# Scores of two heads side by side: queries and keys as fp16 pairs of 64 rows in an attention kernel

## The reference

```python
q = heads(hidden_states @ W_q)                       # (8, 20, 512, 16)
k_t = heads(text_ehs @ W_k)                          # (8, 20, 508, 16)
v_t = heads(text_ehs @ W_v)
scores_t = jnp.einsum('bhsd,bhtd->bhst', q, k_t) * attn_scale
probs_t = jax.nn.softmax(scores_t, axis=-1)
text_out = jnp.einsum('bhst,bhtd->bhsd', probs_t, v_t)
qsem = _l2norm(jnp.einsum('bhst,bte->bhse', probs_t, text_ehs))
sem = jnp.einsum('bhse,bne->bhsn', qsem, _l2norm(ip_ehs))
fused = attn_scores + SEM_SCALE * sem                # attn_scores: q against the 4 image keys
probs_ip = jax.nn.softmax(fused, axis=-1) * spatial_mask[None, None, :, None]
out = (text_out + ip_out) @ W_out + b_out + residual
```

## Time and profile before

| what | value |
|---|---|
| median of three executions | 1642.24 us |
| the profiled execution, its own time | 1642.41 us |
| its span | 1640.5 us |
| mean granted TensorE clock | 0.982 |
| PE busy | 1569.2 us, 96% |
| DVE busy | 1303.0 us, 79% |
| POOL busy | 1258.8 us, 77% |
| ACT busy | 1078.8 us, 66% |
| first and last score matmul (L1593) | 285.0 and 1599.9 us |
| memory read and written by DMA | 68.51 and 34.55 MB |

### The profile page before, as it was taken

The page is one execution under the profiler, slowest core; times in us unless marked ns, Lnnn a source line. Parts: engine busy times, 40 slices in busy tenths (PEclk is TensorE's granted clock), DMA queues, the critical chain, the costliest instruction groups (busy, mean ns, idle before and its releaser), DMA issues.

```text
span 1640.5 us, 39314 instructions
## 1 busy us (share of the span) xinstructions
PE 1569.2 (96%) x13322; PEld 954.5 (58%) x13322; DVE 1303.0 (79%) x3181; ACT 1078.8 (66%) x2308; POOL 1258.8 (77%) x1187
## 2 busy tenths in 40 slices
PE   4999999999999999999999999999999999999996
PEld 2776667555555555555555555555555555555553
DVE  6455454688989977987799789977997899789975
ACT  4465555767777767766777677766776777677762
POOL 4233233788989978997899789977998799879982
PEclk9899999899999999999999999999999999999998
DMA  5455757778789879897889888887888788878973
GB/s 203 133 161 154 200 165 189 150 133 133 137 142 177 154 142 158 149 143 148 156 149 148 149 142 167 144 153 138 155 160 155 139 162 152 155 138 140 153 127 92
DMA packets 656043, 247.89 MB, mean 151 GB/s; under 512 B 619081, under 2 KB 645330, under 8 KB 655858
## 3 DMA queue, kind: packets, MB, share of 16 engines
q1 hardware_dynamic: 654658, 243.75, 77.7%
q10 hardware_dynamic: 1200, 1.80, 0.3%
HBM read 68.51 MB, written 34.55 MB: 63 GB/s over the span
## 4 chain that ended last, share of the span: by engine, by line
PE 76%; DVE 9%; issue 5%; ACT 3%; DMA 3%; POOL 3%; SPq 1%; DVEq 0%; ACTq 0%; POOLq 0%
PE bank L1636 26%; PE bank L1637 16%; PE bank L1689 13%; PE bank L1593 7%; PE bank L1641 3%; PE bank L1603 3%; DVE neg_max L1238 3%; PE bank L1635 3%; DVE probs L1250 2%; DMA late<-wkv 2%; PE bank L1666 2%; PE bank L1750 2%; ACT probs L864 1%; POOL wkv L745 1%; PE bank L1676 1%
## 5 line engine op out<-in xcount | busy, mean ns | idle before, releaser
L1636 PE MATMUL bank<-u_sb,late 127*128 127x508 f16 x2560 | 947.0, 376 | 0.0
L1637 PE MATMUL bank<-u_sb,late 127*128 127x508 f16 (+3 forms) x2560 | 763.9, 298 | 0.0
L1238 DVE TENSOR_REDUCE neg_max<-bank 128x1 f32<-128x508 f32 x640 | 434.3, 679 | 182.2 <-PE bank L1593 181.7
L1635 PE MATMUL bank<-v_ring,late 127*128 127x42 f16 x2560 | 468.0, 183 | 8.8 <-DMA late<-wkv 8.8
L745 POOL TENSOR_TENSOR wkv<-probs,wkv 128x508 f16<-128x508 f32 x320 | 365.4, 1147 | 103.7 <-ACT wkv L876 102.9
L1250 DVE SCALAR_TENSOR_TENSOR probs<-bank,probs 128x508 f32<-128x508 f32 x640 | 431.2, 674 | 5.8 <-PE bank L1637 5.8
L1635 PEld LDWEIGHTS bank<-v_ring,late 127*128 127x128 f16 x2560 | 247.1, 97 | 241.2 <-DMA late<-wkv 11.0
L1636 PEld LDWEIGHTS bank<-u_sb,late 127*128 127x128 f16 x2560 | 248.5, 97 | 187.4 <-issue 3.7
L853 ACT ACTIVATE exp_bias<-neg_max 128x1 f32<-128x1 f32 x512 | 103.8, 203 | 376.0 <-DVE neg_max L1238 373.4
L864 ACT ACTIVATE probs<-bank,exp_bias 128x508 f32<-128x508 f32 x512 | 341.0, 666 | 0.2
L752 POOL TENSOR_TENSOR probs<-probs,wkv 128x508 f32<-128x508 f32 x256 | 290.4, 1145 | 0.0
(11 more groups left out here) (199 smaller groups left out, 1894.9 us busy)
## 6 DMA issues: line engine op xcount, KB each, us to landing
raw<-k_parts SPq DMA_DIRECT2D x192, 79.4 KB, 3.8
raw<-in_ctx_cols SPq DMA_DIRECT2D x8, 1016.0 KB, 7.4
raw<-q_parts SPq DMA_DIRECT2D x32, 240.0 KB, 3.7
v_parts<-v_sb SPq DMA_DIRECT2D x8, 840.0 KB, 11.6
v_ring<-v_parts SPq DMA_DIRECT2D x32, 210.0 KB, 4.1
u_parts<-u_sb SPq DMA_DIRECT2D x8, 825.5 KB, 7.2
u_sb<-u_parts SPq DMA_DIRECT2D x8, 825.5 KB, 5.2
raw<-in_x_cols SPq DMA_DIRECT2D x8, 768.0 KB, 4.4
```

What stands on the lines that cost most here:

```text
L1238: nc.vector.tensor_reduce(neg_max[:, v % 4:v % 4 + 1], bank[s_bank(v)][:, 0:T], AX.X, ALU.max, negate=True)\
L1635: nc.tensor.matmul(o, hi_k, v_ring[0:TP, n, h, k, :], start=(k == 0), stop=False)
L1636: nc.tensor.matmul(y, hi_k, u_sb[0:TP, par, GH[k]:GH[k] + T], start=(k == 0), stop=False)
L1637: done = nc.tensor.matmul(y[:, k * TP:T], hi_k, u_sb[0:TP, par, UL[k]:UL[k] + U_COLS[k]], start=False, stop=(k == TT - 1))
```

## The change

Queries and keys are split into two fp16 parts instead of three bf16 parts. A product then needs four stacked blocks of 16 rows, 64 rows instead of 96. Head h and head h+10 lie in rows 0 to 63 and 64 to 127, and their scores are made by two matmuls in a row, one in each half of the array's rows, into the two score banks. Units now come in pairs: the same 128 query rows of heads h and h+10. So that both matmuls stand together, both wait for the exponentials of all earlier units.

The parts are now split without the scale of the inputs; the scale (`score_unit`, one number per batch) is applied in the exponential, and to the row maximum in the shift. The shift is made for every unit. In phase 1 the second split on ACT and the third on POOL go away, and the queries' parts are stored twice. Groups have four heads instead of five. The table set that holds both exp and log is loaded once by name, and the loads inside phase 2 are gone.

```diff
-    PAIRS = [(0, 0), (1, 0), (2, 0), (0, 1), (1, 1), (0, 2)]
-    KS = len(PAIRS) * D
+    KS = 4 * D
-    GROUP = 5
+    GROUP = 4
+    FAR = H // 2
+    PART_STORES = 3 * NC
...
+        def place(v):
+            pair, rest = divmod(v % OF_BATCH, 2 * ST)
+            return pair + rest % 2 * FAR, rest // 2
...
             def shift(v):
+                b = v // OF_BATCH
                 act.wait_ge(row_max_found, v + 1)
-                nc.scalar.activation(exp_bias[:, v % 4:v % 4 + 1], neg_max[:, v % 4:v % 4 + 1], ACT.Copy, bias=LOG_SCALE)\
-                  .then_inc(bias_ready, 1)
+                nc.scalar.activation(exp_bias[:, v % 4:v % 4 + 1], neg_max[:, v % 4:v % 4 + 1], ACT.Identity, bias=log_col[:, 0:1],
+                                     scale=score_unit[:, b:b + 1]).then_inc(bias_ready, 1)
             def exp(v):
-                if is_turned(v):
-                    act.wait_ge(bias_ready, nth(v) + 1)
-                else:
-                    act.wait_ge(row_max_found, v + 1)
+                act.wait_ge(bias_ready, v + 1)
                 need(act, norms_done, v + 1 - PROB_RING)
-                bias = exp_bias if is_turned(v) else neg_max
                 nc.scalar.activation(probs[:, v % PROB_RING, :], bank[s_bank(v)][:, 0:T], ACT.Exp,
-                                     bias=bias[:, v % 4:v % 4 + 1]).then_inc(probs_ready, 1)
+                                     bias=exp_bias[:, v % 4:v % 4 + 1], scale=score_unit[:, b:b + 1]).then_inc(probs_ready, 1)
...
-                if v < TT and is_turned(v):
+                if v < TT:
                     shift(v)
...
-                if TT <= v + 1 < UNITS and is_turned(v + 1):
+                if TT <= v + 1 < UNITS:
                     shift(v + 1)
...
-                act.wait_ge(bank_drained[j[0]], use(j, b))
-                nc.scalar.activation(parts[0:cn, t, 1, 0:n], resid[0:cn, t % R1, 0:n], ACT.Copy).then_inc(mid_split, 1)
...
-            nc.scalar.activation(unused[:, 1:2], ones[:, 0:1], ACT.Exp)
+            nc.scalar.preload_act_table_set("natural_log_exp_and_others")
...
-                if v < UNITS:
+                if v < TT:
                     row_maximum(v)
+                elif v < UNITS and v % 2 == 0:
+                    row_maximum(v)
+                    row_maximum(v + 1)
...
             def scores(v):
...
-                need(pe, probs_ready, v + 1 - len(S_BANKS))
-                nc.tensor.matmul(bank[s_bank(v)][:, 0:T], q_ring[:, n, h, st * P:(st + 1) * P], k_ring[:, n, h, :],
+                need(pe, probs_ready, v - v % 2)
+                nc.tensor.matmul(bank[s_bank(v)][:, 0:T], q_ring[rows, n, pr, st * P:(st + 1) * P], k_ring[rows, n, pr, :],
                                  start=True, stop=True).then_inc(scores_filled, 1)
...
-                if v + LEAD < UNITS:
+                if v % 2 == 0 and v + LEAD < UNITS:
                     scores(v + LEAD)
+                    scores(v + LEAD + 1)
```

More of the change, by code:

```diff
@@ L489, in store_parts @@
                     c0, cn = CT[t % NC]
[L491 to L494, removed]
+                    job = (Q_JOB + K_JOB)[t]
+                    sp.wait_ge(bank_drained[job[0]], use(job, b))
+                    if t < NC:
+                        dst = q_parts[b].rearrange("(a r) d h s -> r (d h) a s", r=2)
+                        for copy in range(2):
+                            sp.dma_start(dst[copy, c0:c0 + cn], parts[0:cn, t, :, 0:S]).then_inc(parts_saved, 16)
+                    else:
+                        dst = k_parts[b].rearrange("a d h s -> (d h) a s")
+                        sp.dma_start(dst[c0:c0 + cn], parts[0:cn, t, :, 0:T]).then_inc(parts_saved, 16)
             def store_values(b):
@@ L889, in hi @@
                 if nth(v) < 2:
-                    act.wait_ge(parts_saved, 1 + 16 * 2 * NC * B)
+                    act.wait_ge(parts_saved, 1 + 16 * PART_STORES * B)
                 need(act, unit_done, done_before(v, 2))
                 r = pair_of(v)
-                nc.scalar.activation(probs_hi[:, r, :], bank[pt_bank(v)][0:TP, 0:S], ACT.Copy, scale=PROB_SCALE)\
+                nc.scalar.activation(probs_hi[:, r, :], bank[pt_bank(v)][0:TP, 0:S], ACT.Copy)\
                   .then_inc(hi_ready, 1)
@@ L1056, in batch @@
                 if last:
-                    middle(2 * NC - 1)
                     grams(LAST_G_JOB)
@@ L1249, in norm @@
                 dve.wait_ge(quad_filled, v + 1)
-                done = nc.vector.scalar_tensor_tensor(own, y, SQUARE_SCALE if is_turned(v) else 2.0 * PROB_SCALE * SQUARE_SCALE, own,
-                                                      ALU.mult, ALU.mult, accum_out=norms[:, v:v + 1])
+                done = nc.vector.scalar_tensor_tensor(own, y, SQUARE_SCALE if is_turned(v) else 2.0 * SQUARE_SCALE, own,
+                                                      ALU.mult, ALU.mult, accum_out=norms[:, norm_col(v):norm_col(v) + 1])
                 if is_second(v):
@@ L1261, in lo @@
                 r = pair_of(v)
-                nc.vector.scalar_tensor_tensor(probs_lo[:, r, :], bank[pt_bank(v)][0:TP, 0:S], PROB_SCALE, probs_hi[:, r, :],
+                nc.vector.scalar_tensor_tensor(probs_lo[:, r, :], bank[pt_bank(v)][0:TP, 0:S], 1.0, probs_hi[:, r, :],
                                                ALU.mult, ALU.subtract).then_inc(lo_ready, 1)
             def reduce_pair(v):
-                head, pair = v // ST, v % ST // 2
+                far, st = place(v)
+                first = v // OF_BATCH % 2 * H + far - FAR
                 dve.wait_ge(unit_done, v + 1)
-                both = bank[O_BANK + pair][:, 0:2 * VCOLS].rearrange("p (u a c) -> p u c a", u=2, a=2)
-                nc.vector.tensor_reduce(reduced[:, head % (2 * H), 2 * pair:2 * pair + 2, :], both, AX.X, ALU.add).then_inc(pair_reduced, 1)
+                both = bank[O_BANK + st % 2][:, 0:2 * VCOLS].rearrange("p (u a c) -> p u c a", u=2, a=2)
+                nc.vector.tensor_reduce(reduced[:, first:first + FAR + 1:FAR, st, :], both, AX.X, ALU.add).then_inc(pair_reduced, 1)
             def add_residual(b, s, y):
```

134 lines of the change are left out of this document (70 added, 64 removed).

## The result

The changed kernel takes **1817.22 us** (median of 4 runs, 1815.58 to 1818.3) against 1640.84 for the kernel before: ratio 1.107, interval 1.104 to 1.109. It is slower by 176 us. I had forecast 1792, in a range of 1675 to 1860.

What follows compares the result with a forecast made beforehand. PE was taken as the bound before, and a loop through ACT, PE and DVE after, 4.59 us a pair against 4.12: +148, +3 at the start, -1 for tables, +150, so 1792 us, range 1740 to 1850 (8 in 10: 1675 to 1860).

Steps and rivals of the forecast that it cites:

- The new wait: Phase 2: pairs waiting for all earlier exponentials close a loop through ACT, PE and DVE, 3.89 us with old operands.
- The operands: ACT's exponential and shift read added operands from memory, lengthening the loop by 0.20 to 0.60 us a pair; 0.60 taken.
- rival A: The second operand on ACT is free or nearly so: loop 4.09 us, in all 1688 us; chance 0.17.
- What is added to the loop: Phase 2: projections on PE add 0.07 us a pair and DVE's closing work 0.03, on top of 4.49.
- DVE's lumps: DVE's closing work in phase 2, single steps up to 1.51 us, put at 1 us a batch, 0.03 a pair.
- PE's work: Score matmuls side by side in row halves save PE 0.21 us a pair, 3.82 to 3.61, if PE stays the bound.
- Rival B: PE stays the bound, faster: -66 us, about a third held back by DVE and POOL, 1598 us; chance 0.10.
- Cost in phase 2: Pairs at 4.59 us instead of 4.12 over 315.5 pairs cost +148 us, and pairs before unit 0 +3.
- Rival C: PE's stalls in phase 2 lower its clock: about 2080 us; chance 0.07, shared with any other new wait above 1850.
- Tables: Table loads around each logarithm go; those inside phase 2 lay in ACT's room, one at the end saves 1 us.
- Phase 1: ACT loses six roundings and POOL six remainders a batch; taken as 0, with -4 to +4 us.
- Loads: Eight DMAs for a group of four heads instead of ten for five; they stay hidden.

Runs made afterwards that it cites:

- the reordering: The changed kernel with only ACT's order changed, the odd unit's rounding ahead of the even unit's shift: 1689.83 us (1.030).
- single placement: The changed kernel with each unit's score matmuls and row maxima placed one by one, as before the change: 1736.8 us (1.058).
- both repairs: The changed kernel with the scale applied in phase 1 again and the odd unit's rounding ahead of the even unit's shift: 1650.8 us (1.006).

## Why the prediction was right, and where it wasn't

*The new wait* held, step by step. It put the loop with old operands at 3.70 us; the kernel with the pairing alone has 3.71. It put `hi` at 0.47 where it occurs; measured 0.48. That ACT stands still while PE and DVE work, with the rounding still to do, is what the reordering showed. That the loop sets the pace is shown from three sides: undoing the wait, shortening what stands in the loop and swapping its order each give back 80 to 127 us.

*The operands* held. 0.10 was taken for each of two on the exponential and shift, 0.60 a pair; measured 0.09 and 0.18, 4.22 - 3.71 = 0.51 a pair. The mean of loop and `hi` came to 4.41 for 4.49. The second operand was the bound that I left open; rival A, that it is free, fell with the row of 381 ns.

The Trainium skill (ScalarE: Activation LUTs, section What ACT_TABLE_LOAD costs) says about 93 ns for each such operand. The trace agrees, with 0.09 us for the exponential's second operand and 0.18 for the shift's two.

*What is added to the loop* was mis-sized, and this is the largest error of the sum: 0.10 a pair predicted, 0.25 measured. A pair with a projection took 5.33 for a predicted 5.32, and that was luck: the 3.61 in it is the mean over pairs with transposes, where a clean pair counted in the same way has 3.43, and the 0.19 of the next paragraph was missing (3.43 + 0.19 + 1.71 = 5.33). Besides, three of the four stand where the loop takes 4.22 and not its mean, so that 1.11 sticks out instead of 0.83, and the fourth stands on a pair with `hi` (5.87 for 4.70): 4.5 us a batch instead of 3.3. DVE's lumps cost 2.2 instead of 1. And the sum left out ACT's own closing steps, 2.6 us a batch. They had been in the free third of ACT's time, and I never asked what they would cost once ACT was on the path. 0.15 more on 315 pairs is 47 us, and the loop's 0.08 less takes 25 back: by this 4.59 became 4.66, and +148 became +169.

*PE's work* failed, and the result didn't show it. I bounded the second matmul between 0 and 0.22 and took 0, so that a pair came to 3.61. The matmul was indeed nearly free, 0.01 us. But a bound on the matmul itself leaves out what its neighbours pay: 0.19 us for going to 64 rows and back. The pair comes to 3.80, and to 3.84 with what the transposes pay in 2 of 5, not 3.61. For this, and because the loop was shorter, PE waited less than forecast: 0.51 us before a clean pair and not 0.9, and it was 88% busy and not 85. In the measured time this didn't show, because PE was not the bound. It sank the expectation for single placement, by 97 us: some 120 more for the halves, less some 20 that the table set gives and the expectation left out. The one for both repairs already had the 0.19 for clean pairs. Rival B would have been sunk as well: with no loop at all, the pairing could not have saved 66 us, since 3.84 is no less than the 3.82 of before.

*Cost in phase 2*: the start took 7.4 us instead of 3. The first pairs of the changed kernel in the timeline:

```profile
302.98 0.60 PE L1609 MATMUL bank<-raw 64*128 64x508 f16 x2 [3.16 <-ACT probs L887]
...
307.42 0.61 PE L1609 MATMUL bank<-raw 64*128 64x508 f16 x2 [3.83 <-ACT probs L887]
...
313.40 0.39 PE L1609 MATMUL bank<-raw 64*128 64x508 f16 x2
```

PE waited 3.2 and 3.8 us here, and its matmuls ran at the lower of the clock's two levels (0.60 us in place of 0.39; the granted clock is 0.66 between 285 and 307). *Rival C*: past there the clock was 0.98 and 0.99 in the stretches shown above, although PE stood still in most pairs, so the stalls of 0.5 us did not cost the clock.

*Tables*: the sum was right to count -1, since it built the pace from the loop and not from the old time. The reason was wrong. The prediction said that the loads lay in ACT's room before; taken out alone they gave 21 us.

*Phase 1* and *Loads* were rightly put at nothing: the first score matmul of all is at 283.5 where it was at 285.0, and no pair waits for a load.

The forecast of 1792 was 25 us low, inside its own range of 1740 to 1850. Errors of both signs partly made up for each other (operands -0.08, closing work +0.15 a pair).

What stays open: why PE's steps beside a matmul over 64 rows are longer, and the 0.04 us a pair by which closing work passed the forecast when both repairs are in. A kernel with score matmuls over full rows that keeps the two heads apart was not tried.

## What to carry to other kernels

Two things issued together need the storage of both, so pairing across the only two banks turned a chain with a unit of slack into a closed loop; add the loop up from start-to-start rows and compare it with the bound engine's step before asking what the pairing saves. Once an engine is on such a loop, everything it does there counts, its rare closing steps as well, and the order of its instructions can be worth as much as their lengths (here 127 us for one swap). And price a matmul in part of the array with its neighbours: the time from the row ahead to the row behind, not the row alone.

## What the runs showed of the hardware

- A matmul over 64 rows between matmuls over 127 costs PE 0.19 us beside its own work: 0.19 + 0.32 us around it against 0.11 + 0.21 over 128 rows. Before four transposes over 128 rows it costs 0.11 more (0.71 against 0.60 us). Over 96 rows a unit took what it took over 128, 1.82 us. A second matmul over 64 rows right behind the first does not pay again: in the same half it adds 0.21 us.
- Two matmuls of 64 rows and 508 columns take 0.39 us in different row halves and 0.60 in the same.
- An activation of one column took 0.20 us with immediates and 0.38 with two operands from memory; one of 508 columns 669 ns with one and 759 with two.
- Loading a table set took 1.28 us, and sixteen such loads on an engine that was 66% busy, with two more, cost the kernel 21 us.
